# Scores within a chunk as two diagonal 64x64 blocks, and an angle net padded to 128 rows, in a complex state-space mixer with routed experts

## What is computed

```python
zxbcdt = xn @ in_proj_w.T                      # z 512, xBC 640, dt 8
dt = softplus(dt + dt_bias)
xBC = silu(causal_conv4(xBC) + conv_b)         # x 8 heads x 64, B 64, C 64
theta = clip(theta_base + tanh(xn @ theta_w1) @ theta_w2, -pi/2, pi/2)
lam = lambda_base + viscosity_eta * theta**2
log_z = complex(-lam * dt, theta * dt)         # per head, 32 complex states
# chunks of 64 tokens:
A[t, s] = exp(cumlog[t] - cumlog[s]) for s <= t, else 0
S_total = exp(cumlog) * state + sum_s A[t, s] * B[s] * x[s] * dt[s]
y = real(C . S_total) + x * D
g = y * silu(z); g = g * rsqrt(mean(g*g) + 1e-5) * norm_w
mixer = g @ out_proj_w.T                       # 512 -> 256
experts = top-1 of 8 experts (256 -> 256), times its gate
out = x + mixer + experts
```

## Time and profile before

| | |
|---|---|
| median of 3 runs | 1089.71 us (1088.63 to 1090.44) |
| span of the profiled execution, first to last instruction | 1074.8 us |
| own time of the profiled execution | not recorded apart from its span; the median is 14.9 us above the span |
| PE busy | 977.5 us (91%) |
| DVE busy | 923.2 us (86%) |
| ACT busy | 853.5 us (79%) |
| POOL busy | 347.3 us (32%) |
| granted TensorE clock, mean over the span | 0.957 |

### The profile page before, as it was taken

The page is one execution under the profiler, slowest core; times in us unless marked ns, Lnnn a source line. Parts: engine busy times, 40 slices in busy tenths (PEclk is TensorE's granted clock), DMA queues, the critical chain, the costliest instruction groups (busy, mean ns, idle before and its releaser), DMA issues.

```text
span 1074.8 us, 25050 instructions
## 1 busy us (share of the span) xinstructions
PE 977.5 (91%) x8702; PEld 803.8 (75%) x8702; DVE 923.2 (86%) x1487; ACT 853.5 (79%) x1771; POOL 347.3 (32%) x347
## 2 busy tenths in 40 slices
PE   4972699876899999999999999999999999999995
PEld 2532477655688888888888888888888888888884
DVE  5859723259999999999999999999999999999971
ACT  3864212139789999999999999999999999999982
POOL 1210677400213343323222332322333333222332
PEclk9985699996899999999999999999999999999998
DMA  7969587614364665657575656656665657575662
GB/s 244 312 218 394 165 256 208 164 49 155 114 172 142 187 169 165 183 157 200 147 212 149 191 156 191 160 184 186 175 178 164 184 156 202 147 216 136 172 189 58
DMA packets 145986, 193.72 MB, mean 180 GB/s; under 512 B 16862, under 2 KB 106127, under 8 KB 144448
## 3 DMA queue, kind: packets, MB, share of 16 engines
q1 hardware_dynamic: 110656, 146.68, 41.0%
q0 software_dynamic: 24672, 34.36, 16.7%
q10 hardware_dynamic: 10528, 11.01, 3.0%
HBM read 75.99 MB, written 40.63 MB: 109 GB/s over the span
## 4 chain that ended last, share of the span: by engine, by line
PE 63%; ACT 7%; issue 4%; DVE 2%; POOL 2%; DMA 1%; ACTq 0%; POOLq 0%; DVEq 0%
PE ps L900 20%; PE ps L1036 9%; PE ps L980 6%; PE ps L1016 5%; PE ps L1027 5%; PE ps L1044 4%; PE ps L992 3%; PE ps L1005 3%; PE ps L968 3%; PE ps L956 3%; PE ps L926 2%; DVE conv L1380 1%; POOL plus_tile L1590 1%; ACT ps L1166 1%; DMA plus_tile<-x 1%
## 5 line engine op out<-in xcount | busy, mean ns | idle before, releaser
L900 PE MATMUL ps<-early,win 128*128 128x256 f32 x1152 | 275.2, 389 | 11.0 <-DVE theta L1387 6.8
L900 PEld LDWEIGHTS ps<-early,win 128*128 128x128 f32 x1152 | 213.9, 193 | 45.9 <-DVE theta L1387 7.2
L1380 DVE SCALAR_TENSOR_TENSOR conv<-x_pre,col,conv 128x512 f32<-128x512 f32 x240 | 162.6, 741 | 6.4 <-ACT conv L1131 6.3
L1590 POOL DMA_INDIRECT plus_tile<-expert_d,slot_of x64 | 95.7, 1495 | 170.2 <-DMA out<-plus_tile 100.8
L1612 POOL TENSOR_TENSOR rms<-ms,cst 128x1 f32<-128x1 f32 x64 | 52.0, 812 | 250.6 <-ACT ms L1244 250.5
L1036 PE MATMUL ps<-wout,g 128*128 128x256 f32 x512 | 122.9, 383 | 2.5 <-ACT o_tile L1253 2.2
L1036 PEld LDWEIGHTS ps<-wout,g 128*128 128x128 f32 x512 | 93.4, 190 | 18.9 <-issue 7.8
L1596 POOL DMA_DIRECT2D plus_tile<-x x64 | 60.9, 956 | 101.9 <-ACT plus_tile L1237 101.9
L551 POOL DMA_INDIRECT r_tiles<-xn_d,token_of x72 | 68.7, 954 | 71.1 <-POOLq L408 48.5
L1605 POOL DMA_DIRECT2D plus_tile<-o_tile x62 | 67.4, 1092 | 54.6 <-ACT o_tile L1253 42.6
L682 DVE TENSOR_TENSOR r_tiles<-ps,r_expw 128x256 f32<-128x256 f32 x72 | 25.5, 416 | 65.9 <-PE ps L569 63.0
(11 more groups left out here) (172 smaller groups left out, 2237.3 us busy)
## 6 DMA issues: line engine op xcount, KB each, us to landing
cin_s<-cin SPq DMA_DIRECT2D x64, 258.0 KB, 3.1
rep<-bc_d SPq DMA_DIRECT2D x128, 128.0 KB, 3.3
grow_s<-grow SPq DMA_DIRECT2D x64, 256.0 KB, 3.8
bup_s<-bup SPq DMA_DIRECT2D x64, 256.0 KB, 3.0
cown_s<-cown SPq DMA_DIRECT2D x64, 256.0 KB, 2.7
expert_d<-r_tiles ACTq DMA_DIRECT2D x18, 512.0 KB, 3.4
xn_d<-r_tokens SPq DMA_DIRECT2D x16, 512.0 KB, 4.3
xnT_d<-r_turned SPq DMA_DIRECT2D x4, 2048.0 KB, 24.1
```

The costliest lines, as they stand in the source:

```text
L900: last = nc.tensor.matmul(dst, win[:, kt, n * P:(n + 1) * P], xn_in[b][:, kt, :], start=(kt == 0), stop=(kt == KT - 1))
L1380: nc.vector.scalar_tensor_tensor(conv[:, ct, :], x_pre[:, ct, tap:tap + PT], c("conv_w", ct * D_CONV + tap), conv[:, ct, :], ALU.mult, ALU ...
L1590: pool.indirect_dma_start(plus_tile[m % 2][ch][:, :], None, expert_d, bass.IndirectOffsetOnAxis(ap=slot_of[:, t:t + 1], axis=0)).then_inc( ...
```

## The change

`back_own` makes only the two diagonal blocks. In place of one matmul of 128 keys by 128 queries for each head there are two of 64 by 64, one for each chunk. The keys' chunk picks the column half of the array and the partitions of `bank_s`, so that the four matmuls of a head pair use the four quarters of the array, in the tile size (64 x 64) that `back_cross` has already. The block from the second chunk's keys to the first chunk's queries is never written now; VectorE sets `bank_s` to zero once, at the start, and `m_zero` counts to 2. `scored` counts 6 for a tile (`SCORES`): four from `back_own`, two from `back_cross`. In the body for each macro, `back_update` of the tile before moves ahead of `back_own`, so that `back_own` and `back_cross` are neighbours. The angle net's weights and its `hidden` tiles are padded from 49 to 128 rows; the weights with zeros, and `hidden` with ones from a memset that covers all rows.

```diff
-        wl2s = sb("wl2s", [LORA + 1, GROUPS2 * P])
+        wl2s = sb("wl2s", [P, GROUPS2 * P])
...
-        early_hidden = [early_rows(XN_BUFS * KT + 2 * GROUPS2 + b, LORA + 1) for b in range(2)]
+        early_hidden = [early_rows(XN_BUFS * KT + 2 * GROUPS2 + b) for b in range(2)]
...
-                        step(nc.vector.memset(early_hidden[m][32:LORA + 1, :], 1.0))
+                        step(nc.vector.memset(early_hidden[m], 1.0))
...
-            BEFORE = 4
+            SCORES = 6
...
-                    after(sp, s["scored"], 8 * (m - 1))
+                    after(sp, s["scored"], TPM * SCORES * (m - 1))
...
                 def back_own(m, ch):
                     b, t = m % 2, m * TPM + ch
-                    here = slice(ch * P, (ch + 1) * P)
+                    chunks = [slice(ch * P + n * CH, ch * P + (n + 1) * CH) for n in range(CPT)]
...
                     for q in range(PAIRS):
                         for e in range(2):
-                            last = nc.tensor.matmul(bank_s[:, e, q * P:(q + 1) * P], grow_s[b][both(e), place(q), here], cown_s[b][both(e), place(q), here], start=True, stop=True)
-                            if q == PAIRS - 1:
-                                last.then_inc(s["scored"], 1)
+                            for chunk, here in enumerate(chunks):
+                                last = nc.tensor.matmul(bank_s[both(chunk), e, q * P + chunk * CH:q * P + (chunk + 1) * CH], grow_s[b][both(e), place(q), here],
+                                                        cown_s[b][both(e), place(q), here], start=True, stop=True)
+                                if q == PAIRS - 1:
+                                    last.then_inc(s["scored"], 1)
...
-                pe.wait_ge(m_zero, 1)
+                pe.wait_ge(m_zero, 2)
...
                 for m in range(MACROS):
+                    back_update(m, 1)
                     back_own(m + 1, 0)
-                    back_update(m, 1)
                     back_cross(m + 1, 0)
...
-                    dve.wait_ge(s["scored"], 4 * t + 4)
+                    dve.wait_ge(s["scored"], SCORES * (t + 1))
...
                 nc.vector.memset(state_in[0][:, :, :], 0.0).then_inc(m_zero, 1)
-                dve.wait_ge(m_zero, 1)
+                nc.vector.memset(bank_s[:, :, :], 0.0).then_inc(m_zero, 1)
+                dve.wait_ge(m_zero, 2)
```

More of the change, by code:

```diff
@@ L2473 @@
         "x": a["attn_x"].reshape(TOKENS, D_MODEL), "const": const, "halvings": halvings, "cols": cols, "w_in": by_tile(w_in), "w_small": by_tile(w_small),
-        "w_lora1": by_tile(a["attn_theta_w1"]), "w_lora2": lora2, "w_lora2s": lora2s, "w_out": by_tile(a["attn_out_proj_w"].T),
+        "w_lora1": by_tile(a["attn_theta_w1"]), "w_lora2": lora2, "w_lora2s": np.concatenate([lora2s, np.zeros((P - LORA - 1, GROUPS2 * P), np.float32)]), "w_out": by_tile(a["attn_out_proj_w"].T),
         "rows": np.concatenate([a[n].reshape(-1) for n in ("attn_dt_bias", "ffn_router_b", "attn_lambda_base", "attn_viscosity_eta")])[None, :],
```

## The result

The changed kernel takes 1080.65 us (median of 4 runs, 1079.65 to 1082.52); the kernel before takes 1089.76 us beside it. The ratio is 0.9919 with a 95% interval of 0.9905 to 0.9933. The forecast was 1083.8 us with a range of 1078.5 to 1088.5. The profiled execution has a span of 1077.8 us and a time of its own of 1079.65 us.

A forecast was written before the change was run, and what follows sets the result against it. TensorE never waits, but VectorE's work limits how far a period can shrink, so only its waits for TensorE come off. -4.6 - 0.9 - 1.4 + 1.0 = -5.9 us gives 1083.8 us, range 1078.5 to 1088.5.

The forecast's parts named there:

- the early waits go too: Rival, 225 to 406 us: VectorE's waits of 1.57 and 1.36 us vanish as well; -8.8 us, 1080.9 us, chance 0.09.
- the four terms: 406 to 1024 us -4.6, 225 to 406 us -0.9, 1024 us to the end -1.4, new memset +1.0 us.
- The price of the blocks: TensorE's L980 and L992 together: 1.02 us a tile with four array tiles at a time, a gain of 0.68 us.
- The angle net: L926 and the group behind it on TensorE: 2.98 becomes 2.60 us, 0.38 us less for each macro.
- The steady part: 406 to 1024 us: VectorE's 12 waits for TensorE go, -4.6 us, bounds 0 and -5.3.
- Where TensorE will wait instead: TensorE gets 3.0 us of slack in a period, held mostly by ScalarE, in many short pauses.
- The early waits: 225 to 406 us: waits of 0.4 and 0.54 us go, 1.57 and 1.36 stay; -0.9 us, bounds 0 and -3.9.
- The memset: Ahead of the mixer's matmuls: zeroing 1024 PSUM columns takes 1.1 us, hardly covered; +1.0 us, bounds +0.9 and +1.2.
- The end: 1024 us to the end: two pairs of L980 and L992 in TensorE's chain, -1.4 us, bounds -0.5 and -2.3.
- my slower rival: Slack gathers in one long TensorE pause each period and the granted clock falls; 1103 us, chance 0.06.
- a sign of being wrong: After 406 us in the mixer: a granted clock under 1.00, one of three listed signs against the forecast.
- The 14.9 us "around the span": Kernel before: profiled span 1074.8 us, median 1089.7 us; the difference was taken to lie around the span and left.

The follow-up runs named there:

- Two variants on another chip: Changed kernel with the blocks' chunk loop outermost, 1075.01 us (ratio 0.9977); changed kernel without the matmuls of the scores across chunks, 1076.47 us (0.9996).
- the last experiment: Changed kernel with later wait for the zeroed bank, macro 5's gather earlier, rms ahead of gather in the loop and once in the prologue: 1063.9 us, ratio 0.9893.

## Why the prediction was right, and where it was not

- **The number, and luck.** 1080.65 us lies in the stated range, 3.1 us under the forecast, and all but on the 1080.9 us of the rival "the early waits go too". On the chip where the changed kernel was run again the ratio is 0.9990; applied to 1089.7 us that is 1088.6, just outside the range. That the time fell inside is owed in part to the chip. The forecast's own range, 1080.5 to 1087, doesn't follow from the bounds of the four terms either: these add up to 1079.1 and 1090.4 us.
- **What bounds the kernel.** Right: TensorE, with VectorE 0.5 us below it. Masking halved in the kernel before left its period at 50.37 us; less TensorE work in any form gave 49.89 to 49.95, and 49.9 was forecast. VectorE's idle time is 0.03 us in 618.
- **The price of the blocks.** Right: 1.08 us for L981 and L994, where 1.02 was forecast from four at a time. This was the term with the widest choice, as no row had shown four at a time. It didn't matter: the padding alone gives the same period.
- **The angle net.** 0.96 + 1.73 = 2.69 us, where 2.60 was forecast. TensorE is busy for 48.1 us of a period (28.76 + 19.34), where "about 47" was: its groups came out 0.4 us a period dearer (4 x 0.06 + 2 x 0.09), and some 0.8 us I can't place.
- **The steady part.** Twelve waits, -4.6 us in 618 us or 0.37 a period, was the forecast; 11 periods gave -5.3, or 0.48 each. Right in kind, and a little small: over 618 us 0.48 a period makes 5.9 us, past the bound of 5.3. VectorE's idle time was 0.39 us a period there (4.28 us from tile 12 to 56). The other 0.09 fits the 0.08 us by which the records of two neighbouring VectorE instructions overlap when nothing stands between them, an estimate from the timelines.
- **Where TensorE waits instead.** "Mostly ScalarE" was said, at 3.0 us a period. It is VectorE: L1018 waits for the masking L1479, 18.2 us in 23 waits of at most 0.9 us, and TensorE's idle time is 1.8 us a period (19.8 us from tile 12 to 56). Short and many they are, but for the one of 3.2 us near the end.
- **The early waits: the step that failed.** "I keep both" was said of the waits of 1.57 and 1.36 us. Both went, and with them ScalarE's share of the waits, which the forecast had left out. Before, VectorE waited from 225 to 440 us as follows, and the changed kernel shows none of these three:

```profile
DVE g L1498 <- PE ps L1027: 3.5, 3, 1.6
DVE frac L1423 <- ACT frac L1181: 1.7, 3, 1.1
...
DVE att L1477 <- PE ps L992: 0.4, 1, 0.4
```

  The first two make 5.2 of the 6.3 us from tile 0 to 12; the third, at 276.2 us, lies ahead of tile 0. I had taken "TensorE had itself waited for VectorE or ScalarE just before" as a sign that TensorE wasn't the cause. The likely cause is that these engines had waited for TensorE in their turn: its lateness went round and came back as their waits. This was the rival "the early waits go too", priced at 1080.9 us. That the waits went is shown, the circle is argued from the rows; padding alone kept one wait of 1.6 us and gained 4.3 of the 6.3. The rival's price was met in part by luck: it had 3.8 us for this stretch, and the waits that it left out were offset by the memset and the end.
- **The memset.** +1.0 was forecast, +1.9 came. The memset itself is 1.12 us; most of the rest is the granted clock behind a longer pause.
- **The end.** -1.4 was forecast, +1.1 came (56 to 63). GpSimd, ScalarE and TensorE near 1018 us:

```profile
1014.15 3.39 POOL L1593 DMA_INDIRECT plus_tile<-expert_d,slot_of  x1 [0.30 <-issue]
1017.53 2.37 POOL L1615 TENSOR_TENSOR rms<-ms,cst 128x1 f32<-128x1 f32 x1
...
1019.93 0.47 ACT L1255 ACTIVATE o_tile<-ps,rms 128x256 f32<-128x256 f32 x1 [1.91 <-POOL rms L1615]
...
1020.55 3.32 PE L1038 MATMUL ps<-wout,g 128*128 128x256 f32 x8 [3.23 <-ACT o_tile L1255]
```

  The gather and the rms are held, ScalarE is late, TensorE pauses for 3.23 us, and the next group takes 3.32 us, where it takes 1.73 (the clock over 1016 to 1030 us was 0.88). That is the mechanism of my slower rival, once and not in every period; a clock under 1.00 after 406 us was named as a sign of being wrong, and here it came. With the rms ahead of the gather this stretch takes 39.6 and 39.4 us in the two profiles that have it (42.1 without, 39.6 with, on one chip).
- **The 14.9 us "around the span".** Wrong, and without effect on a difference: they were an expert stage shorter by 13 us in that execution.
- **What I had not thought of at all.** A VectorE without gaps slows GpSimd. I costed GpSimd at nothing, as its work was untouched and its share 32%. Its gathers went from 1.39 to 2.35 us on average (440 to 990 us). On the chip where the changed kernel was run again the ratio was 0.9990 in place of 0.9919. One gather of 9.74 us is the largest piece of that: moving it gave back 4.6 us, and the rms and gathers behind it are the likely rest. Two variants on another chip have the same gather of 9.74 us. In the profile of the result, and for reasons that no row shows, it went through; its other executions weren't profiled.

In sum -5.3 - 6.3 + 1.9 + 1.1 = -8.6 us where -5.9 was forecast: the early waits make more than the whole difference (-5.4), the steady part adds -0.7, and the memset (+0.9) and the end (+2.5) take over half of it back.

## What to carry to other kernels

When two engines are within 1% of each other, look first at the smallest edit that takes the slower one below the other: here a padding of 49 rows to 128 gave the steady gain alone, and the blocks only added slack. If the engine that ended a wait had itself waited just before, that doesn't prove it innocent; follow the circle back once more. And before you close the gaps of VectorE, ask what GpSimd does with them: put what others wait for (here the rms) ahead of what may be held up (the gather), and what may be held ahead of a long wait; two such edits in GpSimd's order and one later wait were worth 8.4 us (1075.59 to 1067.17) on a chip where the change alone was worth nothing. Then look whether the moved instruction is held in its new place: here a gather was, for 9.7 us in each period, and it cost nothing only because nobody waited for it.

## What the runs showed of the hardware

- **GpSimd is held while VectorE works without gaps.** In the changed kernel's profile 49 of 62 gathers from 240 us on took over 1.3 us (1.09 us is one that is not held). The longest were 9.74 us, in three profiles, and a rms (0.55 us alone) was held for up to 5.76 us. With VectorE relieved by half of the masking the mean gather fell from 2.35 to 1.32 us. A held one can stay out over a run of 12 VectorE instructions (409.76 to 417.59 us, above) and not only one.
- **What lets it in: mostly a VectorE instruction that reads PSUM.** Held gathers end about 1.04 us after the start of some VectorE instruction. In the changed kernel 43 of the 49 end 0.9 to 1.1 us after the start of L1479 or L1500, with an input in PSUM, the other six after that of an L1382, with both inputs in SBUF. The short holds say little: of the 30 gathers over 1.3 us in the kernel before 23 end so behind the start of an instruction with two inputs in SBUF. The long ones say more: in the fourteen profiles 201 of 212 gathers of over 3 us end 0.85 to 1.3 us after the start of an instruction with an input in PSUM, though many of these are the same place of a period over and over. It is no rule without exceptions, as one of 5.17 us in the last experiment ended behind an instruction with two inputs in SBUF. I did not try the kind of operand by itself. The Trainium skill (SBUF — State Buffer, section "SBUF: two separate sides") has a mechanism: VectorE and GpSimd share a port pair that one of them holds exclusively for a whole instruction, and a VectorE instruction with two SBUF inputs needs it against a GpSimd instruction that reads SBUF. The long holds agree with it: in the one of 9.74 us above VectorE's instructions from 409.76 us on have two inputs in SBUF. But for the descriptors of a DMA from GpSimd's queue the Trainium skill, in the same section, names only VectorE's modes that use two ports, and says that tensor_tensor didn't stall a DMA; here gathers were held over tensor_tensor and scalar_tensor_tensor in fp32.
- **The same schedule, two outcomes.** Issued 0.67 us after the same VectorE instruction in both, the same gather took 1.91 us in one execution and 9.74 in another.
- **Four array tiles at a time.** The 16 blocks of 64 x 64 (32 records) start 0.51 us before the next group, where two at a time would take 0.82 us by the price of L992 and L1027 (an estimate). Two column halves over the same rows (L1005, 0.61 us) overlap as well as two row halves do (L992, 0.61 us).
- **The expert stage has two lengths,** about 13 us apart, with one program; the kernel before takes 1075 to 1077 us on three chips and 1089 on another, a difference of that size.
